# Attention scores in one four-bank stage, fewer waits on TensorE, and new orders in a one-core graph network kernel

## What is computed

```python
h  = x @ W0 + b0;            x = LN(x + (adj @ h) / adj.sum(-1))             # layer 0
w  = (x @ Wq1 * (adj @ (mask * x @ Wk1))).sum(-1) / 16
x  = LN(x + softmax(w over nodes) * (x @ Wv1))                              # layer 1
q, k, v = heads(x @ Wq.T + bq), heads(x @ Wk.T + bk), heads(x @ Wv.T + bv)  # 8 heads of 32
s  = einsum('bhqd,bhkd->bhqk', q, k) * 32**-0.5 * (adj + adj)               # the scores
x  = LN(x + merge(softmax(s) @ v) @ Wo.T + bo)                              # layer 2
h  = LN(relu(hyper(x, W1, b1)));  x = LN(x + hyper(h, W2, b2) + x)          # layer 3
```

## Time and profile before

| | us |
|---|---|
| median of three runs (lowest, highest) | 1862.93 (1862.92, 1864.81) |
| the profiled execution, its own time | 1865.63 |
| its span in the profile | 1863.9 |
| PE busy | 1818.8 (98%) |
| DVE, ACT, POOL busy | 1450.0, 1447.0, 1440.7 (77 to 78%) |

### The profile page before, as it was taken

The page is one execution under the profiler, slowest core; times in us unless marked ns, Lnnn a source line. Parts: engine busy times, 40 slices in busy tenths (PEclk is TensorE's granted clock), DMA queues, the critical chain, the costliest instruction groups (busy, mean ns, idle before and its releaser), DMA issues.

```text
span 1863.9 us, 55098 instructions
## 1 busy us (share of the span) xinstructions
PE 1818.8 (98%) x15357; PEld 1607.8 (86%) x15357; DVE 1450.0 (78%) x3909; ACT 1447.0 (78%) x4463; POOL 1440.7 (77%) x2857
## 2 busy tenths in 40 slices
PE   6899999999999999999999999999999999999997
PEld 5788888888888888888888888888888888888886
DVE  5687787877787877887877877877878777878775
ACT  3777788877788877888877888777888777888776
POOL 3677887777887777887778877778877778877775
PEclk8999999999999999999999999999999999999998
DMA  4011001111011111011110011110011110111100
GB/s 129 7 41 41 17 22 39 39 39 39 7 32 39 39 39 37 3 39 39 39 39 28 11 39 39 39 39 17 23 39 39 39 39 6 34 39 39 37 20 13
DMA packets 95435, 62.96 MB, mean 34 GB/s; under 512 B 10288, under 2 KB 94768, under 8 KB 95408
## 3 DMA queue, kind: packets, MB, share of 16 engines
q1 hardware_dynamic: 93648, 60.73, 11.0%
q10 hardware_dynamic: 1760, 1.90, 0.3%
HBM read 45.82 MB, written 16.78 MB: 34 GB/s over the span
## 4 chain that ended last, share of the span: by engine, by line
PE 95%; DVE 2%; ACT 1%; issue 1%; SPq 1%; DMA 0%; POOL 0%; DVEq 0%; POOLq 0%; ACTq 0%
PE ps L418 55%; PE ps L521 6%; PE ps L489 6%; PE ps L481 6%; PE ps L497 4%; PE ps L403 3%; PE ps L434 3%; PE ps L510 3%; PE ps L471 2%; PE ps L428 2%; PE ps L455 2%; DVE z L949 1%; PE ps L408 1%; ACT z L647 0%; SPq L381 0%
## 5 line engine op out<-in xcount | busy, mean ns | idle before, releaser
L647 ACT ACTIVATE z<-z,z_max 128x128 f32<-128x128 f32 x1024 | 398.5, 397 | 0.0
L737 POOL TENSOR_TENSOR ln_rs<-ln_ve,minus_half 128x1 f32<-128x1 f32 x640 | 352.2, 550 | 50.1
L757 POOL TENSOR_TENSOR z<-z,z_rcp 128x1024 f32<-128x1024 f32 x128 | 243.0, 1898 | 39.6 <-DVE z_rcp L967 39.5
L740 POOL TENSOR_SCALAR ln_nm<-ln_mv,ln_rs 128x1 f32<-128x1 f32 x640 | 169.9, 266 | 109.7 <-POOL ln_rs L737 109.7
L586 ACT ACTIVATE h<-h,ln_nm,ln_rs 128x512 f32<-128x512 f32 x128 | 104.5, 817 | 143.7 <-POOL ln_nm L740 141.4
L735 POOL TENSOR_TENSOR ln_ve<-ln_mv,eps_col 128x1 f32<-128x1 f32 x640 | 122.2, 191 | 119.4 <-DVE ln_mv L873 119.1
L418 PE MATMUL ps<-w1T,txT 128*128 128x512 f32 x768 | 209.5, 408 | 1.0 <-DVE txT L883 1.0
L418 PE MATMUL ps<-w2T,mnT 128*128 128x256 f32 x1536 | 205.3, 282 | 0.0
L949 DVE SCALAR_TENSOR_TENSOR z<-ps,a_hold 128x512 f32<-128x512 f32 x256 | 174.1, 681 | 37.5 <-PE ps L481 33.9
L418 PEld LDWEIGHTS ps<-w2T,mnT 128*128 128x128 f32 x1536 | 192.6, 188 | 9.2 <-issue 0.2
L647 ACT ACTIVATION_READ_ACCUMULATOR z<-z,z_max 128x1 f32 x1024 | 199.4, 195 | 0.0
(11 more groups left out here) (152 smaller groups left out, 5045.9 us busy)
## 6 DMA issues: line engine op xcount, KB each, us to landing
x_in<-in_x_dram SPq DMA_DIRECT2D x128, 128.0 KB, 2.1
a_hold<-in_adj_dram SPq DMA_DIRECT2D x128, 128.0 KB, 2.2
out_dram<-y_out SPq DMA_DIRECT2D x128, 128.0 KB, 1.9
a_in<-in_adj_dram SPq DMA_DIRECT2D x128, 64.0 KB, 1.9
x<-in_L_gnn_Wqk_dram ACTq DMA_DIRECT2D x1, 512.0 KB, 5.6
h<-in_L_gnn_W_dram SPq DMA_DIRECT2D x1, 512.0 KB, 5.2
h<-in_L_gnn_W_dram ACTq DMA_DIRECT2D x1, 512.0 KB, 10.2
v<-in_L_gnn_Wo_dram SPq DMA_DIRECT2D x1, 256.0 KB, 6.3
```

Of the source, the lines that this page charges most:

```text
L647: m = act.activation(z[:, g % 2, h, :], z[:, g % 2, h, :], ACT.Exp, bias=z_max[:, g % 2, h:h + 1], accum_out=z_sum[:, g % 2, h:h + 1])
L737: pool.tensor_tensor(rs[n][:, g:g + 1], ve[n][:, g:g + 1], minus_half[:, :], ALU.pow).then_inc(root_made[n], 1)
L740: pool.tensor_scalar(nm[n][:, g:g + 1], mv[n][:, g, 0:1], rs[n][:, g:g + 1], -1.0, ALU.mult, ALU.mult).then_inc(shift_made[n], 1)
L757: pool.tensor_tensor(zg, zg, z_rcp[:, g % 2, :].unsqueeze(2).to_broadcast([P, HEADS, P]), ALU.mult)\
```

## The change

1. `sc0` and `sc1` become one stage `sc` with four banks. For each half of the features it multiplies on rows 0, 32, 64 and 96 in turn. VectorE reads all four banks with one multiplication (`z`, 128x1024). The two maxima stay two instructions.
2. TensorE's waits go through `need`, which leaves out a wait for a count that an earlier wait on the same semaphore has covered. The wait for a bank's earlier owner is left out too where TensorE has already begun a stage that follows from that owner's data (`FOLLOWS`, `begun`).
3. All orders and banks are new, for every engine. Among others the projection `q1` of a group moves from the end of one pass to the second place of the next.

```diff
-         "x2t": 1, ..., "mp": 1, "sc0": 2, "sc1": 2, "pt": 2,
+         "x2t": 1, ..., "mp": 1, "sc": 4, "pt": 2,
...
+FOLLOWS = {"at": ("ax",), "ax": ("h0",), "h0": ("x1t", "amx"), "x1t": ("xg", "v1"), ...
+           "v2": ("cx",), "mp": ("tx", "mn"), "sc": ("pt",), "pt": ("cx",), "cx": ("wo",),
+           "wo": ("tx",), "tx": ("h1",), "h1": ("mn",), "mn": ("y",)}
...
+            group, passed, begun = {}, {}, set()
+            def need(semaphore, ahead, g=None):
+                count = ahead + 1 if g is None else ahead * G + g + 1
+                if passed.get(semaphore.name, -2 * G) < count:
+                    passed[semaphore.name] = count
+                    q = group["now"] + ahead
+                    pe.wait_ge(semaphore, q + 1 if g is None else nth(q, g))
...
-            def sc(half):
-                def stage(q, g, o, b):
-                    for s in ("q0", "q1", "k0", "k1"):
-                        pe.wait_ge(read[s], q + 1)
-                    for c in range(C):
-                        for k in range(RG // 2):
-                            r = half * RG // 2 + k
+            def sc(a, g, o, b):
+                for s in ("q0", "q1", "k0", "k1"):
+                    need(read[s], a)
+                for c in range(C):
+                    for r in range(RG):
...
                 for (stage, g, ahead, b), owners in zip(schedule, bank_turns(schedule, previous)):
                     for other, og, away in owners:
-                        q = it + away
-                        pe.wait_ge(read[other], q + 1 if other in per_group else nth(q, og))
+                        later = ((s, 0 if s in per_group else og, away) for s in FOLLOWS.get(other, ()))
+                        if not any(s in begun for s in later):
+                            need(read[other], away, None if other in per_group else og)
...
-            def z_(half):
...
+            def z_(q, g, o):
+                dve.wait_ge(made["sc"], nth(q, g))
+                dve.scalar_tensor_tensor(out=z[:, g % 2, :, :].rearrange("p (r c) n -> p r (c n)", r=RG),
+                                         in0=ps[:, b:b + RG, 0:C * P], scalar=HC,
...
-        at.0+:5 at.1+:3 v2.1:4 sc1.0:0 sc0.0:6 v2.2:2 at.2+:0 ax.0+:3 sc1.1:1 mp.2:5 at.3+:0 ax.1+:3 h0.0+:4
+        at.0+:4 q1.0:2 at.1+:0 ax.0+:5 mp.2:7 at.2+:6 sc.0:1 at.3+:5 ax.1+:7 v2.1:0 mp.3:6 sc.1:1 ax.2+:0
```

More of the change, by code:

```diff
@@ L32 @@
 BANKS = {"at": 1, "ax": 1, "h0": 1, "x1t": 1, "amx": 1, "xg": 1, "wt": 1, "pb": 1, "v1": 1,
-         "x2t": 1, "q0": 1, "q1": 1, "k0": 1, "k1": 1, "v2": 1, "mp": 1, "sc0": 2, "sc1": 2, "pt": 2,
+         "x2t": 1, "q0": 1, "q1": 1, "k0": 1, "k1": 1, "v2": 1, "mp": 1, "sc": 4, "pt": 2,
          "cx": 1, "wo": 1, "tx": 1, "h1": 1, "mn": 1, "y": 1}
@@ L61 @@
[L61 to L65, removed]
@@ L359, in load_hold @@
             def load_hold(q, g):
-                after(sp, read["sc0"], before(q, g, G))
-                after(sp, read["sc1"], before(q, g, G))
+                after(sp, read["sc"], before(q, g, G))
                 sp.dma_start(a_hold[:, g, :, :], adj_d[bass.ds(q * G + g, 1)].rearrange("g n m -> n g m").to_broadcast([P, C, P]))\
@@ L398, in _, with ax @@
         def _(pe):
-            def ax(q, g, o):
-                pe.wait_ge(x_loaded[g], q * 16 + 16)
-                pe.wait_ge(read["at"], nth(q, g))
+            group, passed, begun = {}, {}, set()
[5 more added lines that the diff above has]
+                    pe.wait_ge(semaphore, q + 1 if g is None else nth(q, g))
+            def ax(a, g, o):
+                pe.wait_ge(x_loaded[g], (group["now"] + a) * 16 + 16)
+                need(read["at"], a, g)
                 for c in range(C):
@@ L404, in ax, with at @@
                 return m
-            def at(q, g, o):
-                pe.wait_ge(a_loaded[g], q * 16 + 16)
+            def at(a, g, o):
+                pe.wait_ge(a_loaded[g], (group["now"] + a) * 16 + 16)
                 return pe.transpose(o[:, 0:P], a_in[:, g, :], ident[:, :])
@@ L522, in mn, with y @@
                 return m
-            def y(q, g, o):
-                pe.wait_ge(read["mn"], nth(q, g))
+            def y(a, g, o):
+                need(read["mn"], a, g)
                 return rows3(o[:, 0:D], lambda i, c: mnT[:, i, g % 2, c, :], lambda i, c: w2T[:, i, c, :], C2)
+            counted_by_group = {read[s].name for s in per_group} | {s.name for s in (amT_made, wm_made, hb_made, col_made)}
             stages = {"at": at, "ax": ax, "h0": h0, "x1t": x1t, "amx": amx_, "xg": xg, "wt": wt, "pb": pb, "v1": v1,
@@ L531, in _ @@
                       "mn": mn, "y": y}
-            wide = {"sc0": sc(0), "sc1": sc(1), "pt": pt}
+            wide = {"sc": sc, "pt": pt}
             def walk(schedule, it, previous):
+                group["now"] = it
+                for name in passed:
+                    passed[name] -= 1 if name in counted_by_group else G
+                begun.clear()
+                begun.update((stage, g, ahead - 1) for stage, g, ahead, _ in previous)
                 for (stage, g, ahead, b), owners in zip(schedule, bank_turns(schedule, previous)):
                     for other, og, away in owners:
-                        q = it + away
-                        pe.wait_ge(read[other], q + 1 if other in per_group else nth(q, og))
-                    q = it + ahead
-                    m = wide[stage](q, g, ps[:, b, :], b) if stage in wide else stages[stage](q, g, ps[:, b, :])
+                        later = ((s, 0 if s in per_group else og, away) for s in FOLLOWS.get(other, ()))
+                        if not any(s in begun for s in later):
+                            need(read[other], away, None if other in per_group else og)
+                    m = wide[stage](ahead, g, ps[:, b, :], b) if stage in wide else stages[stage](ahead, g, ps[:, b, :])
                     m.then_inc(made[stage], 1)
+                    begun.add((stage, g, ahead))
             pe.wait_ge(set_ident, 2)
@@ L608, in run @@
                     act.wait_ge(made[stage], q + 1)
-                    after(act, made["sc0"], q * G)
-                    after(act, made["sc1"], q * G)
+                    after(act, made["sc"], q * G)
                     act.activation(dst, o, ACT.Identity, bias=bias).then_inc(read[stage], 1)
```

221 lines of the change are left out of this document (111 added, 110 removed), and 2 rows, old and new, of the table FOLLOWS.

## The result

The changed kernel takes 1875.57 us (median of 4 runs, 1874.08 to 1877.16) beside 1862.97 us of the kernel before on the same chip (4 runs). The ratio is 1.0063, with a 95% interval of 1.0048 to 1.0078: slower by 0.6%, three times what can be told from no change. The forecast was 1815.5 us with a range to 1850, so the result lies outside it, on the side that had a chance of 5%.

The account below looks back on a forecast made before the run. TensorE, busy 98% of the span, was taken as the bound. Terms of -1.70, -0.74, -0.34 and +1.25 gave -1.53 us a pass, 47.4 us over 31 passes: 1815.5 us, range 1775 to 1850.

Parts of the forecast that it names:

- pt.0: TensorE's wait for GpSimd's first softmax product: chain 8.1 us against 8.5 of TensorE work, taken as 0.1 a pass.
- term D: New TensorE waits in the new order, at four places with little room: +1.25 us a pass, bounds +0.53 and about +3.
- Term A: Score stretches on TensorE: 4.38 us a pass becomes four stages of 0.67, 2.68 in all; -1.70 a pass.
- Term B: TensorE's waits fall from 212 to 98 a pass, so 54% of 1.37 us issue idle goes: -0.74 a pass.
- Term C: The old order's wait of cx for the copy of pT goes: -0.34 us a pass.
- cx.0: TensorE's wait for ScalarE's pT copy: at least 0.53 us, plus 0.25 if four exponentials ahead end late; taken 0.78.
- ax.3: TensorE's wait for a bank of the second score stage: 4.47 us against 4.21 of work, 0.26, taken 0.2 a pass.
- x1t.0: TensorE's wait for a bank of the scores issued just ahead of cx.0: 2.04 us against 1.87, taken 0.17.
- `q1` priced at nothing: q1 moves to the head of the next pass; in the loop it only shifts, a miss being some tenths of a us.
- The DMAs priced at nothing: Loads and stores move by whole steps on a queue whose engines are 11% busy; claimed to cost nothing.
- The second: Rival: PSUM banks bound each of four score stages, 0.3 more at each; -0.5 us a pass, 1847 us; chance 15%.
- The fourth: Rival: ScalarE's exponentials delay every pT copy, all four cx wait 1.3; +2.9 us a pass, 1953 us; chance 4%.

Follow-up runs that it names:

- e8: e6 with SyncE's list issuing all four loads of x for two groups ahead before the stores; 1842.16 us, ratio 0.9873 to the kernel before.
- e1: The changed kernel with GpSimd's step hT moved from ahead of three xb to behind probs.0; 1917.17 us, ratio 1.029 to the kernel before.
- e7: e6 with GpSimd's hT moved back behind the LayerNorm roots, just ahead of probs.2; 1873.21 us, ratio 1.0042 to the kernel before.
- e6: e5 with two edits behind the loop: q1.0 in bank 7, and probs.0 ahead of dinv.0 and x2c.3; 1857.78 us.
- e2: The kernel before, stages, orders and banks kept, with covered TensorE waits left out (103 a pass, not 212) and remaining bank-owner waits reordered; 1856.59 us.
- e4: The changed kernel with score multiplications on rows 0 and 32 twice, then 64 and 96 twice; 1877.21 us, ratio 1.0072 to the kernel before.
- e3: The changed kernel with every TensorE wait issued, none left out as covered; 1881.43 us, ratio 1.0094 to the kernel before.
- e5: The changed kernel with all four xb ahead of am and hT in GpSimd's list; 1858.89 us, ratio 0.9969 to the kernel before.
- e9: e8 with hT moved behind all four products, ahead of c3, and VectorE's ecnt moved to just ahead of wmax; 1916.07 us, ratio 1.0271.

## Why the prediction was wrong

**The step that failed** is the sentence "The new orders of GpSimd, 80% busy in a pass, and of ScalarE, 80%, are covered by TensorE as long as the loop stays above some 50 us", and with it the line for `pt.0` in term D, taken at 0.1. The share of busy time says that GpSimd has 11 us a pass to spare. It doesn't say where. For `pt.0` I walked the chain of one graph's data (scores, `z`, exponentials, reciprocal, product) and summed 8.1 against 8.5. I did not walk the list in which that product stands. What it takes was there: `hT` could not start before `mp.3`, behind it three `xb` (736 ns each in the trace of the kernel before) and 0.8 us of `dmax` were listed ahead of `probs.0`, and the diff shows that order. The place cost 1.4 us a pass more than a covered `h0` (PE's own waits there are 1.3). GpSimd's list is 1.1 of it (e8 against the changed kernel) and the chain itself 0.3 (what e1, e7 and e8 leave there, 1.11 against 0.8). 31 times 1.1 is 34 us, and e8's median lies 33 us under the changed kernel's (35 with each against the kernel before on its own chip), one or two of them from the end as in e6.

The walk of the chain was off as well, in both its sums. Behind `ax.3` the list has four products ahead of `pt.0` (`h0.1`, `v2.2`, `v2.3`, `h0.2`), and I counted five. TensorE's work from the start of `sc.0` to the end of `h0.2` took 8.2 (915.88 to 923.29, and 0.8), with the wait at `ax.3` in it, not 8.5; the chain, where nothing of GpSimd's stands in front of it (e8), took 8.6, not 8.1. That is the 0.3.

Point by point:

- **Term A** (-1.70) held by its own measure: the four stages take 0.66, 0.65, 0.67 (with the wait for `cx` behind it put into D) and 0.67, 2.65 for the forecast 2.68. Its reason was right only in part: e2 shows that 0.6 of it is waits between halves, and could be had without the new stage. And it isn't the four row groups in turn that make two halves fit into 0.67, since e4 takes 0.69 or less with two at a time; that a half alone takes 0.64 stays without a cause.
- **Term B** (-0.74) was too large. e2 measures 0.2 a pass, e3 0.17. The idle of PEld put down to issue fell from 18.2 to 15.4 us in ten passes, by 15% and not by 54%. Counting waits doesn't price them. That most of them stood where TensorE's sequencer was ahead anyway fits this, but no run separates them. The kernel before had two more rows of this kind, which I had not used:

```profile
PEld ps L428 <- issue: 2.8, 10, 0.3
PEld ps L418 <- ACT v L578: 2.6, 10, 0.3
PEld ps L497 <- issue: 1.7, 10, 0.2
```

- **Term C** (-0.34): the old wait is gone, replaced by the one in D, as said.
- **Term D** (+1.25) had the right places. `cx.0` took 0.5 (1.17 for the stage ahead of it instead of 0.67), not 0.78: the added block of exponentials cost nothing. `ax.3` took 0.3 (1.09 from `h0.0` instead of 0.8) for 0.2, `x1t.0` 0.3 for 0.17, `pt.0` 1.4 for 0.1. In all 2.5. (The 0.17 was worked out with 0.53 for the wait at `cx.0`; with the 0.78 that the sum takes it would have been nothing.) The multiplication over four banks took 1223 ns for the forecast 1.22:

```profile
L970 DVE SCALAR_TENSOR_TENSOR z<-ps,a_hold 128x1024 f32<-128x1024 f32 x128 | 156.5, 1223 | 63.3 <-PE ps L498 61.5
```

- **`q1` priced at nothing.** In the loop TensorE stands about 0.2 ahead of `sc.0` for its copy (the third `at` takes 0.33 to the next start, a free one 0.11), "some tenths" as written. Behind the loop it is not free: the last pass and the end hold 3.8 us more, with waits for its bank, its copy and `probs.0` in the timeline. Bank and order gave 1.7 back in e6; the rest was not tested.
- **The DMAs priced at nothing** cost nothing in the changed kernel as it stands. They cost 0.6 a pass once GpSimd's list is mended: `h0.2` to `pt.0` is 1.71 in e5 and 1.11 in e8.
- **Together**: -1.70 and -0.34, then +2.5 and +0.2 give +0.7 a pass; measured is +0.23. The 0.4 to 0.5 between them is what was won in places that were not walked; the issue idle (0.28 less) and the old wait for `v` (0.26, above) are of that size. That split is read from idle sums and was not tested by a run.
- **The rivals.** The second had the banks as the bound. The waits for `z` did come, at `ax.3`, `x1t.0` and one `amx`, but at 0.6 us a pass by TensorE's starts they take a third of term A and not all of it. The Trainium skill, page "TensorEngine Tiling (Array Packing)", section "Gotcha 1: PSUM Pressure", says that row tiling raises the pressure on PSUM; the trace agrees, with these 0.6 us. The fourth, on the losing side, was a queue: the right kind of mechanism on the wrong engine, ScalarE's `cx` where it was GpSimd's `pt.0`. D came to 2.5, near its criterion of 2.78, and more than half of that is one wait.
- **The range.** With D at 0.8 the sum gives 1801 and not 1795 as the low end of the forecast's own range. The result lies on the other side, so this changes nothing.

With GpSimd's and SyncE's lists mended the pass is 55.6 and the time 1842.16, inside the range given and still 27 us over the forecast. The stages and the waits of the change are a gain; its order on two helpers' queues took more than the gain away.

## What to carry to other kernels

An engine that is 80% busy is not slack in front of a given step. For each step that the critical engine waits for with little room, walk two things: the chain of its data, and everything listed ahead of it on its own queue, with what the head of that queue waits for; then take the later. When you move a step out of the way, look who stands behind its new place, since in a dense stretch the same 2 us are paid again, in whole or in part (e1, e7, e9), in e1 and e9 with a lower clock on top, while steps that are ready cost nothing in a gap that was there anyway (e5, e8), provided their loads were issued a pass ahead.

## Of the hardware

The granted clock is one thing I had not expected here. It is 1.00 in the pass shown of the kernel before and of the changed one, though TensorE stands there for 1.33 and, 1.7 us of work later, for 0.45. In e1, with a wait of 0.48 and then one of 1.64 within 4.4 us, it fell to about half for 3.4 us and came back by itself, in about two passes of three; each time the pass took 1.2 to 1.4 us more. That comes on top of the wait. The length of a single wait doesn't decide it. The passes of e1 that escaped have the same waits, as this one, in which the clock stayed at 1.00:

```profile
944.41 0.64 PE L513 MATMUL ps<-pT,v 128*32 128x128 f32 x16 [0.49 <-ACT pT L676]
946.69 0.41 PE L447 MATMUL ps<-ident,x 128*128 128x128 f32 x2 [1.64 <-ACT x L609]
```

In e9 it fell in one pass of three, behind waits of 0.6 and 1.1, both shorter than the 1.33 of the changed kernel. What decides it stayed open.

The second is the price of waits between score stages: sixteen matmul instructions took 1.10 with eleven waits in front of and among them and 0.73 with fewer, on the same data and banks (e2). Over a whole pass the waits left out were worth about 0.2 (e3, e2), so it is the place of a wait that has a price, not the wait.
